# Expert tiles in three parts between the filter's steps, and a table of its own for the gather

## What is computed

```python
xn = _layernorm(x)
x = x + L0_attn(xn) + L0_ffn(xn)     # a Mamba filter with a chain of norms and projections; 2 of 8 experts per sequence
xn = _layernorm(x)
x = x + L1_attn(xn) + L1_ffn(xn)     # causal attention, 16 heads of 64, rotated q and k; experts per token
```

```python
logits = jnp.einsum('btd,de->bte', X, Wg) + bg
topv, topi = jax.lax.top_k(logits, S)            # S = 2
w = jax.nn.softmax(topv, axis=-1)
xs = X[:, :, None, :] * w[..., None]
for e in range(E):                               # E = 8, hidden size 512
    h = jax.nn.silu(xs @ W1[e]) * (xs @ W3[e])
    y = h @ W2[e]
    out = out + jnp.where(topi == e, y, 0.0).sum(axis=2)
```

## Time and profile before

| | |
|---|---|
| median of 3 runs | 2759.58 us (2758.66 to 2765.24) |
| the profiled execution's own time | 2747.9 us |
| its span, first to last instruction | 2746.1 us |
| busy time PE, DVE, ACT, POOL | 2175.3, 1657.5, 1195.3, 920.4 us |
| granted TensorE clock, mean | 0.861 |

### The profile page before, as it was taken

How to read it: one execution, slowest core, us unless ns; L and a number is a source line. 1 busy time by engine, 2 the same in 40 slices (tenths; PEclk the granted TensorE clock), 3 DMA queues, 4 the chain that set the end, 5 groups by cost and what they waited for, 6 DMA issues and landing times.

```text
span 2746.1 us, 38800 instructions
## 1 busy us (share of the span) xinstructions
PE 2175.3 (79%) x11640; PEld 1518.3 (55%) x11640; DVE 1657.5 (60%) x2929; ACT 1195.3 (44%) x2702; POOL 920.4 (34%) x581
## 2 busy tenths in 40 slices
PE   4257789878898788978789778987888877888985
PEld 1033456655665566655566556655566555665665
DVE  2965775556754776557765577556775477654432
ACT  2223554345633455345543455433563435524641
POOL 0321671027510374005720176103741047301601
PEclk8568888897899888898899878998789978899997
DMA  2000011311222111321113112121122211131223
GB/s 94 0 15 1 31 53 56 115 49 42 74 82 75 49 44 59 102 80 36 55 64 103 59 35 71 68 99 47 38 69 91 78 43 54 51 119 70 72 93 114
DMA packets 82452, 175.06 MB, mean 64 GB/s; under 512 B 11448, under 2 KB 42560, under 8 KB 81984
## 3 DMA queue, kind: packets, MB, share of 16 engines
q1 hardware_dynamic: 78144, 164.05, 17.6%
q0 software_dynamic: 4096, 8.40, 1.1%
HBM read 123.71 MB, written 15.14 MB: 51 GB/s over the span
## 4 chain that ended last, share of the span: by engine, by line
PE 48%; issue 16%; DVE 15%; POOL 11%; ACT 6%; DMA 2%; SPq 1%; DVEq 0%; POOLq 0%; ACTq 0%
PE G L926 8%; PE G L1048 6%; PE G L1033 4%; DVE HS L1527 4%; POOL Y L1943 3%; POOL REG L1954 3%; POOL YG L1968 2%; PE FC L1010 2%; PE G L937 2%; PE FM L1022 2%; PE G L1065 2%; PE FM L738 2%; POOL REG L1957 2%; PE FM L896 2%; ACT REG L1330 2%
## 5 line engine op out<-in xcount | busy, mean ns | idle before, releaser
L1048 PEld LDWEIGHTS G<-REG 128*128 128x128 f32 x2560 | 386.0, 217 | 71.4 <-issue 51.2
L1048 PE MATMUL G<-REG 128*128 128x64 f32 x2560 | 390.2, 290 | 3.1 <-DVE REG L1833 3.1
L1527 DVE TENSOR_TENSOR_SCAN HS<-DA,D 128x1024 f32<-128x1024 f32 x128 | 351.0, 2742 | 19.3 <-ACT DA L1209 18.7
L1943 POOL TENSOR_TENSOR Y<-Y,HC 128x1024 f32<-128x1024 f32 x114 | 274.5, 2408 | 240.1 <-DVE HC L1549 239.8
L1033 PE MATMUL G<-ident,REG 128*128 128x128 f32 x1280 | 260.7, 307 | 110.7 <-ACT REG L1330 109.4
L926 PEld LDWEIGHTS G<-XGT,MW 128*128 128x128 f32 x1920 | 294.7, 239 | 54.6 <-issue 54.6
L926 PE MATMUL G<-XGT,MW 128*128 128x128 f32 x1920 | 301.1, 324 | 18.9 <-DMA MW<-moe 18.9
L1954 POOL TENSOR_TENSOR REG<-REG,cos_t 128x512 f32<-128x512 f32 x128 | 183.0, 1430 | 378.7 <-ACT REG L1306 378.0
L1330 ACT ACTIVATE REG<-G 128x128 f32<-128x128 f32 (+3 forms) x512 | 222.9, 435 | 198.6 <-PE G L1033 194.8
L1033 PEld LDWEIGHTS G<-ident,REG 128*128 128x128 f32 x1280 | 162.8, 161 | 155.2 <-issue 125.0
L1022 PE MATMUL G<-REG 64*128 64x128 f32 (+3 forms) x768 | 237.5, 523 | 7.4 <-POOL REG L1957 6.4
(11 more groups left out here) (287 smaller groups left out, 3955.8 us busy)
## 6 DMA issues: line engine op xcount, KB each, us to landing
MW<-moe SPq DMA_DIRECT2D x120, 768.0 KB, 4.2
REG<-ROT SPq DMA_DIRECT2D x256, 128.0 KB
EW<-experts SPq DMA_DIRECT2D x16, 514.5 KB, 4.2
XG<-x_rows SPq DMA_DIRECT2D x8, 960.0 KB, 5.5
y_rows<-YO SPq DMA_DIRECT2D x120, 64.0 KB, 1.5
X<-xT SPq DMA_DIRECT2D x8, 256.0 KB, 5.8
W<-weights SPq DMA_DIRECT2D x1, 2048.0 KB, 9.4
REG<-xT SPq DMA_DIRECT2D x8, 256.0 KB, 2.7
```

Of the source, the lines that this page charges most:

```text
L1048: mm = pe.matmul(G[3][:, col:col + DK], PT[:, n % 2, c * P:(c + 1) * P], V[:, c, j * P + h * DK:j * P + (h + 1) * DK], start=c == 0, stop= ...
L1527: dve.tensor_tensor_scan(HS[:, :, :].rearrange("p h s -> p (h s)"), DA[:, n % 2, :, :].rearrange("p h s -> p (h s)"), D1[:, :, :].rearrang ...
L1943: pool.tensor_tensor(Y[:, :, :], Y[:, :, :], HC_EARLY if early else HC[:, n % 2, :, :], ALU.add).then_inc(y_add.sem, 1)
```

## The change

The work of an expert tile is split in three parts: gate, up and down. `TOKEN_PARTS` lists the 45 parts in the order in which PE ran them before, and the table `PARTS_AFTER` says how many of them follow each filter step (steps -1 to 28). Before, tiles 1 to 14 stood whole behind some of the steps, by `t_share`. The gate half has a semaphore of its own, `gg_mm`, for which the tanh waits in place of `ug_mm`; DVE's second product waits for `ug_mm`. The gather reads its row numbers from a second table, `place_kept`, which DVE fills at step 19 of phase 2 (`keep_places`), and `number_places` no longer waits for `ys_d`. The order of functions on ACT leaves the number of its table loads as it was.

```diff
-        weight = [0.5 if 18 <= p <= 21 else 1.1 for p in range(F_STEPS)]
-
-        def t_share(p):
-            return 1 + round(sum(weight[:p]) / sum(weight) * (MOE_TILES - 1))
+        TOKEN_PARTS = [("gate", 0), ("up", 0)]
+        for i_ in range(1, MOE_TILES):
+            TOKEN_PARTS += [("gate", i_), ("up", i_), ("down", i_ - 1)]
+        TOKEN_PARTS.append(("down", MOE_TILES - 1))
+        PARTS_AFTER = (0,1,2,1,2,1,2,1,2,1,2,1,2,2,2,1,2,1,2,1,1,1,1,2,2,1,2,1,2,1)
...
-            PHASE_1 += [("t", u) for u in range(t_share(p), t_share(p + 1))]
+            PHASE_1 += [("t", u) for u in TOKEN_PARTS[part_:part_ + PARTS_AFTER[p + 1]]]
...
-            def token_use(b, i, following):
-
-                up_gate(b, i)
-                if i:
-                    down(b, i - 1)
-
-            def up_gate(b, i):
+            def token_use(b, part, i, following):
+
+                if part == "gate":
+                    gate_rows(b, i)
+                elif part == "up":
+                    up(b, i)
+                else:
+                    down(b, i)
+
+            def gate_rows(b, i):
...
-                g = 2 * (i % 2)
-                for half in range(2):
-                    for c in range(CHUNKS):
-                        at = half * HID + c * P
-                        mm = pe.matmul(G[g + half][:, c * P:(c + 1) * P], MW[:, i % SLOTS, at:at + P], XGT[:, i, :], start=True, stop=True)
+                for c in range(CHUNKS):
+                    mm = pe.matmul(G[2 * (i % 2)][:, c * P:(c + 1) * P], MW[:, i % SLOTS, c * P:(c + 1) * P], XGT[:, i, :], start=True, stop=True)
+                mm.then_inc(gg_mm.sem, 1)
+
+            def up(b, i):
+                for c in range(CHUNKS):
+                    at = HID + c * P
+                    mm = pe.matmul(G[2 * (i % 2) + 1][:, c * P:(c + 1) * P], MW[:, i % SLOTS, at:at + P], XGT[:, i, :], start=True, stop=True)
                 mm.then_inc(ug_mm.sem, 1)
...
-            def token_use(b, i, following):
-
-                act.wait_ge(ug_mm.sem, ug_mm.at(b, i + 1))
+            def token_use(b, part, i, following):
+
+                if part == "down":
+                    rows_done(b, i)
+                if part != "gate":
+                    return
+                act.wait_ge(gg_mm.sem, gg_mm.at(b, i + 1))
...
-            def token_use(b, i, following):
-
+            def token_use(b, part, i, following):
+
+                if part != "up":
+                    return
...
+                dve.wait_ge(ug_mm.sem, ug_mm.at(b, i + 1))
                 dve.wait_ge(sx_d.sem, sx_d.at(b, i + 1))
...
             def number_places(b):
 
-                dve.wait_ge(ys_d.sem, ys_d.at(b - 1))
                 dve.wait_ge(xg_in.sem, xg_in.at(b - 1))
                 dve.wait_ge(place_d.sem, place_d.at(b, 11))
                 dve.tensor_copy(place_i[:, :, :].rearrange("p k t -> p (k t)"), places[:, 56:64]).then_inc(place_d.sem, 1)
+
+            def keep_places(b):
+
+                dve.wait_ge(ys_d.sem, ys_d.at(b - 1))
+                dve.tensor_copy(place_kept[:, :, :].rearrange("p k t -> p (k t)"), places[:, 56:64]).then_inc(kept_d.sem, 1)
...
-                    pool.wait_ge(place_d.sem, place_d.at(t))
+                    pool.wait_ge(kept_d.sem, kept_d.at(t))
```

More of the change, by code:

```diff
@@ L376, in build @@
                  d1_mm, d2_mm, lg_mm, wb_mm, e1_mm, e2_mm, v_mm, pj_mm, sc_mm, pt_mm, pv_mm, ot_mm, wo_mm, gl_mm,
-                 xtok_mm, rank_mm, xt_mm, ug_mm, dn_mm, yt_mm] + [n.by_pe for n in norms]
+                 xtok_mm, rank_mm, xt_mm, gg_mm, ug_mm, dn_mm, yt_mm] + [n.by_pe for n in norms]
         by_act = [biased, u_silu, r_silu, soft, da_exp, qsq_d, ksq_d, q_gelu, g_act, d1_gelu, rt_act,
@@ L381, in build @@
                   gk_d, lni_d, hsm_d, m1_d, h2_d, m2_d, l0a_d, xm_d, rt_d, wb_d, yf_d, l0f_d, x2_d, xn2_d, rot_d,
-                  nm_d, rec_d, o_d, x3_d, gt_d, pick_d, place_d, sx_d, hh_d, out_d] + [n.by_dve for n in norms]
+                  nm_d, rec_d, o_d, x3_d, gt_d, pick_d, place_d, kept_d, sx_d, hh_d, out_d] + [n.by_dve for n in norms]
         by_pool = [du_d, skip_y, y_add, y_gate, xnb_d, rope_d, xw_d, ys_d]
@@ L390, in build @@
         X_AFTER = {0: 1, 1: 2, 2: 3, 6: 4, 7: 5, 8: 6, 10: 7, 11: 8, 15: 9, 16: 10, 18: 11}
-        weight = [0.5 if 18 <= p <= 21 else 1.1 for p in range(F_STEPS)]
-        def t_share(p):
-            return 1 + round(sum(weight[:p]) / sum(weight) * (MOE_TILES - 1))
+        TOKEN_PARTS = [("gate", 0), ("up", 0)]
[3 more added lines that the diff above has]
+        PARTS_AFTER = (0,1,2,1,2,1,2,1,2,1,2,1,2,2,2,1,2,1,2,1,1,1,1,2,2,1,2,1,2,1)
+        assert len(PARTS_AFTER) == F_STEPS + 1 and sum(PARTS_AFTER) == len(TOKEN_PARTS) - 2
         EARLY = 2
         EARLY_AT = {23: ((0, 0),), 24: ((0, 1),), 25: ((0, 2), (1, 0)), 26: ((1, 1),), 27: ((1, 2),)}
-        PHASE_1 = [("o", 0), ("x", 0), ("t", 0), ("f", -1)]
+        PHASE_1 = [("o", 0), ("x", 0), ("t", TOKEN_PARTS[0]), ("t", TOKEN_PARTS[1]), ("f", -1)]
+        PHASE_1 += [("t", u) for u in TOKEN_PARTS[2:2 + PARTS_AFTER[0]]]
+        part_ = 2 + PARTS_AFTER[0]
         for p in range(F_STEPS):
             PHASE_1.append(("f", p))
-            PHASE_1 += [("t", u) for u in range(t_share(p), t_share(p + 1))]
+            PHASE_1 += [("t", u) for u in TOKEN_PARTS[part_:part_ + PARTS_AFTER[p + 1]]]
+            part_ += PARTS_AFTER[p + 1]
             if p in X_AFTER:
@@ L1082, in phase_1 @@
                 each_step(b, t, f, filter_step, token_use, front_start, attention_end, early_scan)
-                if t is not None:
-                    down(t, MOE_TILES - 1)
             def phase_2(b, f, t):
@@ L1347, in phase_1 @@
                 each_step(b, t, f, filter_step, token_use, front_start, lambda t, b: None, early_scan)
-                if t is not None:
-                    rows_done(t, MOE_TILES - 1)
             def phase_2(b, f, t):
@@ L1876, in phase_2 @@
                         number_places(b)
+                    if s == KEEP_AT:
+                        keep_places(b)
                     if f is not None:
@@ L1968, in gather @@
                 pool.indirect_dma_start(out=YG[:, k, c, :], out_offset=None, in_=y_rows,
-                                        in_offset=bass.IndirectOffsetOnAxis(ap=place_i[:, k, c:c + 1], axis=0)).then_inc(yg_in.sem, 16)
+                                        in_offset=bass.IndirectOffsetOnAxis(ap=place_kept[:, k, c:c + 1], axis=0)).then_inc(yg_in.sem, 16)
             def add_picks(t):
```

9 lines of the change are left out of this document (5 added, 4 removed).

## The result

The changed kernel takes 2547.39 us, the median of four runs (2532.6 to 2564.83), beside 2759.35 us for the kernel before in the same session: a ratio of 0.923, 95% interval 0.9164 to 0.9296. That is 212 us less, where 140 were forecast; the stated range ended at 2560 us, some 200 less than before. The profiled execution took 2555.12 us and spans 2553.3.

The account below looks back on a forecast made before the run. TensorE was taken as nearest the bound, losing idle time and half clock. Terms -96 - 9 - 33 - 1 - 1 = -140 us gave 2619 us; own range 2585 to 2655, wider range 2560 to 2690.

Parts of the forecast that it names:

- Phase 1, -96 forecast: Filter and experts of six full laps: splitting tiles into parts saves 16 us per lap (ends 6 and 24), -96 us.
- The walked lap: Phase 1 lap from 1102.2, priced row by row in the new order at full clock: the projection L1010 26.1 us earlier.
- waits for weights: Expert tiles in phase 1: two or three waits of up to 1 us for weight loads, within the 8 us kept.
- I keep half of it, 8 us: Phase 1: of about 14 us of TensorE busy time lost to half clock per lap, 8 us is assumed to remain.
- The last lap, -9: Phase 1 of the lap without a front, 21.2 us idle: 9 us less, between 4 and 16.
- The table, -33 forecast: Attention: the copy into place_i no longer waits for GpSimd's sum; 5.5 us (ends 2 and 8.8) in six laps.
- so at most 8.8: Attention: upper bound on the table's gain, second lap's 182.4 us against the first's 173.6, without stall or gathers.
- the 131 named: Sign of being right: phase 1 of a full lap at 131 us, TensorE idle 15 to 18, clock 0.90 or more.
- wrong signs: TensorE waiting for MW in most tiles, VectorE waiting for up parts, a falling clock, or an equal GpSimd wait behind the copy.
- parts in the way: Rival, phase 1: a 0.9 us part behind every step delays ready ones, half clock stays; -75 us, 2684 us, chance 0.21.
- Full clock: Rival, phase 1: with less idle time TensorE stays at 2.4 GHz; 198 us less, 2561 us, chance 0.15.
- the 2.3 weighed: Attention: the added copy can cost a lap 2.3 us each time it meets a GpSimd addition; total about 14 us less gain.

Follow-up runs that it names:

- projection first: Projections put ahead of the second head's transposes on TensorE in the attention; in the changed kernel 2531.8 us (0.9212 to before), in the kernel before 2712.65 us (0.9851).
- gate 0 twice: The changed kernel with the gate half of tile 0 multiplied twice, same output: 2552.37 us, 0.9269 to before; the same edit in the kernel before: 2729.48 us, 0.9916.

## Why the prediction was off

Two terms of the sum were too small: phase 1 by 26.5 us over the six laps and phase 2 by 28.8. With the last lap as forecast, they are all but a few us of what the traces show beyond the 140.

**Phase 1, -96 forecast, -122.5 measured.** The order of the steps and their places held. The walked lap is the third of the kernel before and starts at 1102.2. The lap shown after is the fourth, at 1332.0, the longest of its six (127.9 us); the third, at 1040.9, took 125.7. Forecast gains, all at full clock, against those measured in the lap shown and in the third: q 5.1 us against 5.2 and 5.2; the transposes 12.0 against 9.0 and 10.3; the expert matmul 15.6 against 11.0 and 11.7; the mean 19.5 against 13.9 and 16.3; the projection 26.1 against 21.1 and 23.3. The shortfall is half clock, as foreseen (2.04 to 2.08 us rows behind waits of 1.38 and 1.94), and the waits for weights; the two are not told apart.

The step that failed is "I keep half of it, 8 us", which takes a loss of TensorE's busy time for a loss of the lap. The busy time did grow by as much: the walk's 122.9 us with some 15 idle leave 108 busy (an estimate), and 116.3 were measured. But the six laps average 126.5 us, only 3.6 over the 122.9, and TensorE's idle time shrank to 10.2 us in place of the 15 to 18 named. With 3.6 in place of 8 the term is 26.1 - 3.6 - 2.1 = 20.4 us a lap, as measured.

What half clock costs a lap can be read from laps of one trace. A lap of the kernel before, to set beside the 149.0 us of the earlier trace rows, and then two laps of the changed kernel's second trace:

```profile
777.70:923.60 145.90, 119.42 (x620) 87.48 (x619) 78.67 (x192) 50.07 (x79) 10.77 (x6) 0.89 0.26 86
```

```profile
1037.50:1162.80 125.30, 114.28 (x620) 82.83 (x618) 78.16 (x192) 50.07 (x81) 8.99 (x6) 0.95 0.30 100
...
1924.20:2050.50 126.30, 117.09 (x620) 85.88 (x618) 78.20 (x192) 50.09 (x81) 9.02 (x6) 0.92 0.29 100
```

In both pairs one lap has some 7 us more at half clock. Before, TensorE was busy for 3.1 us longer and the lap took 3.1 us longer: all of it reached the lap, although TensorE was idle for 26.5 us of it. After, busy time grew by 2.8 us and the lap by 1.0. So a rate read from the kernel before did not hold for the changed one, and it is not the amount of idle time that decides. Why the changed kernel absorbs more is not shown; the likely reading is that more of its half clock falls on expert parts that stand in front of a wait.

**The last lap, -9.** Measured 9.1. The last attention, forecast at 1, gave 1.7, and the experts alone, also forecast at 1, gave 0.1.

**The table, -33 forecast, -61.8 measured in six laps.** The mechanism was right: no wait before the copy, and 0.16 us instead of 2.13. The size failed: 5.5 us a lap were forecast and 10.3 measured, more than the bound "so at most 8.8". The first lap's attention is no bound, because its own length depends on the clock: it took 163.2 to 175.9 us over the traces of these kernels, and 168.3 in the kernel before. (the earlier trace rows are also cut some 4 us later; cut at the first expert matmul, as here, the same difference is 178.4 - 168.3 = 10.1.) What the table is worth depends on the course. By the means given above it is 4.2 us without the long drop and 6.4 with it, some 6 at the five slow laps in six of the kernel before, so the 5.5 was near for a fixed mix. With projection first, where no full lap has the long drop, it is (1016.8 - 988.5) / 6 = 4.7 us, if the split has no part in that. In slow laps the earlier copy also changes the half clock behind it: from 64 us on, the clock's record has 31 us of it in the lap of 1896.4 and 20 in the lap of 871.8. The forecast put nothing for a change of course. Two attentions of the changed kernel took the slow course instead of five, which at the 4.8 us between its two means is 2.4 us a lap (an estimate); the rest is spread within a course. How much of that the table causes and how much is luck of the mix is left open; three of six with the table alone, four with the split alone and two in each trace of the changed kernel do not tell, and the changed kernel with gate 0 twice has the same sum with four.

**The signs.** Phase 1 came out 4.5 us shorter than the 131 named, the clock at 0.92 as asked, the projection within 1.5 us of its input, the copy without a wait; the attention fell by 10.3 us a lap where the sign asked for 5.5 or so. Of waits for weights two or three of up to 1 us were forecast; the lap shown has two, 0.5 us at tile 9 and 1.9 at tile 13. TensorE's idle time, 10.2 us, is under the 15 to 18 named. Of the wrong signs one came, in small: VectorE waits for an up part once a lap, 3.1 us. The rivals: parts in the way did not happen. Full clock, at 2561 us, was nearest in time, but for the wrong reason, as the clock did not stay up.

**The copy beside GpSimd.** The second copy met a GpSimd addition in two laps of eight. VectorE's copy, and then GpSimd in the same 4 us:

```profile
388.12 2.59 DVE L1821 CAST place_kept<-places 128x8 uint32<-128x8 f32 x1
```

```profile
387.10 2.36 POOL L1964 TENSOR_TENSOR Y<-Y,HC 128x1024 f32<-128x1024 f32 x1
389.40 1.27 POOL L1975 TENSOR_TENSOR REG<-REG,cos_t 128x512 f32<-128x512 f32 x1
```

The copy ends at 390.71, with the second of them at 390.67. By the rule of the Trainium skill, "SBUF — State Buffer", "Who interferes with whom", it should wait for whole instructions of GpSimd, and this trace agrees. It waited for the second addition too, though that began 1.3 us after the copy. At one meeting in four this costs 0.6 us a lap, not the 2.3 weighed. How often they meet hangs on the timing: with projection first the same copy is long in seven laps of eight (its duration in ns, min/median/max):

```profile
L1824 DVE CAST place_kept<-places x8: 159/3279/3289, 378.9 to 2381.2; 128x8 uint32<-128x8 f32 x8
```

## What to carry to other kernels

Where two engines' work alternates on one engine, cut the filler into pieces no longer than the replies it fills, and free the last steps of a phase of it; here that was worth 20 us of a 147 us lap, some 15 by spreading and 3 to 5 at the end. When pricing a clock loss, do not take TensorE's lost busy time for the lap's: find two laps of one trace that differ in it. Here 3.1 us of busy time cost the lap 3.1 us in one kernel, and 2.8 us cost it 1.0 in the other. And when a stretch that an edit does not touch gets faster, look at the granted clock and at the variants that do useless work before crediting the edit.

## What was not expected of the hardware

One program's attention has two courses, told apart by whether the granted clock falls for 14 us at 33 us into it. In the same trace of one kernel the two took 167 and 178 us, but half clock elsewhere makes the lengths overlap over the traces. Ahead of the long fall stands a wait of 1.73 us on TensorE, and one of 1.57 us lies across its start. The kernel before nearly always repeats the slower course (four of its six attentions take 178.4 to 178.6 us). That is the likely reason why useless work could pay 0.8%, and why an edit that leaves the attention alone took 58 us out of it in its trace. The mixes also widen the runs: 2532.6 to 2564.83 for the changed kernel, and 2737.13 to 2776.37 in 16 runs of the kernel before, whose first three had lain within 0.3%. What decides on entry which course a lap takes is open.
